# First attention: weighted-value calls placed one at a time behind score and projection calls, with new orders on all four engines

## The chip, the cores and the metric

One core of a Trainium2 chip runs the whole program. The metric is device time in microseconds, the median of several executions.

## What is computed

The reference is a two-layer transformer with modulated layer norms. Only its first attention is touched by the change. It works on 32 samples of 256 tokens by 128 features, with 16 query heads and 8 key heads of 64 features (two query heads share one key head):

```python
h = _layernorm(x) * (1 + ca) + sa
x1 = _rmsnorm(h, norm_w)
q, k, v = heads(x1 @ Wq), heads(x1 @ Wkv[:, :512]), heads(x1 @ Wkv[:, 512:])
q, k = _mh_rmsnorm(q, q_gamma), _mh_rmsnorm(k, k_gamma)     # per head
sim = tanh(q @ k.T / 50) * 50 / sqrt(64)                     # causal mask
out = sum over the two query heads of softmax(sim) @ v       # per key head
x = x + ga * (merge(out) @ Wout)
```

A mixture-of-experts layer, a second attention and a second feed-forward part follow. They are the same before and after the change.

## The kernel before

The function `attention0` (L297) holds the stage. Its unit of work is one **sample** n: two tiles (t = 0, 1) of 128 tokens. Each engine runs a loop over n written out by hand, in which it works on several samples at once: while the scores of sample n are made, the projections of n+2, the transposes of n+1 and the end of n-1 are done. There is no order except the one written in these loops, and each engine executes its own list strictly in that order. Semaphore waits (`wait_ge`) in each helper tie the engines together. The steps of a sample are these:

- **TensorE** (PE). `pe_transpose_x` turns the modulated input, `pe_project_qk` (L432, m = 0 to 5) and `pe_values` (L402) multiply with the weights (float32, 512 columns). `pe_turn_k` (L444) and `pe_turn_q` (L460) turn keys and queries, eight float16 transposes each. `pe_scores` (L476) makes the score products of one of four **groups** g of four query heads in the three-bank PSUM tile `pS`, as eight float16 calls of 512 or 256 columns. `pe_weighted_values` (L491, L492) makes the weighted values of one **pair** p of query heads (two pairs to a group): six float32 calls, whose stationary operand is a 128x128 block of the probabilities `pr` and whose moving operand is `va`, 66 columns wide (64 values and the row sum). A float32 matmul shows in the trace as two records, each with its own weight load. `pe_heads_back` (L513), `pe_out_project` (L529) and `pe_out_back` (L543) end the sample.
- **ScalarE** (ACT). `act_square_qk` (L869) squares a projection, `act_hi` (L879) makes the high float16 half of the normalised keys (u = 0) or queries (u = 1), `act_take_values` (L922), `act_take_k` (L885) and `act_take_heads` (L909) copy from PSUM, `act_tanh` (L897) and `act_exp` (L903) work on one group of scores.
- **VectorE** (DVE). `dve_gain` (L698) applies the gammas, `dve_sums` (L704) and `dve_factors` (L719 to L738) make the inverse norms, `dve_norm` (L745) multiplies them into `qg`, in SBUF, in place. `lower` (L759) makes the low float16 half: of keys on VectorE, of queries on GpSimd, each reading the high half that ScalarE made. `dve_outputs` (L750, L754) divides a pair by its row sums, `dve_take_q` (L767) copies turned queries from PSUM, `dve_normalise` (L680) and `dve_ln` (L638 to L652) prepare later samples, `dve_add` (L128) and `dve_measure` (L136, L140) end an earlier one.
- **GpSimd** (POOL). `gp_mask` (L982) sets the masked probabilities of a group to zero in two instructions, `gp_sum` (L990) adds the two query heads of a pair, `lower` (L759) makes the low half of the queries, and `gp_modulate` (L998, L1000) the modulated input.
- **SyncE** (SP) copies the turned keys into a second tile with the halves exchanged (`k2`, L373 and L374), for which the scores wait.

In the order before, all six calls of a pair stand in one block:

```python
for gg in range(G2):
    hh = p % 2 * G2 + gg
    for t in range(TT):
        out = pO[p % 2][:, (t * G2 + gg) * VW:(t * G2 + gg + 1) * VW]
        pe.matmul(out, w[:, hh * N + t * P:hh * N + (t + 1) * P], v[:, 0, p, :], start=True, stop=t == 0)
    last = pe.matmul(out, w[:, HPG * N + hh * P:HPG * N + (hh + 1) * P], v[:, 1, p, :], start=False, stop=True)
last.then_inc(s_pv, 1)
```

and the scores of a group are followed by both pairs of the same group. On VectorE, the lower half of the keys and the normalising of a later sample come in the order `dve_outputs(n, 1)`, `dve_normalise(n + 3)`, `lower(n + 1, 0, 0)`, `lower(n + 1, 0, 1)`. On ScalarE the high half of the keys comes first and that of the queries after it; on GpSimd `lower(n + 1, 1, 0)` and `lower(n + 1, 1, 1)` have the mask of group 2 between them.

## Time and profile before

| | us |
|---|---|
| median of 3 runs | 2014.13 (2013.62 to 2015.25) |
| profiled execution, first to last instruction | 2010.0 |
| median less that span | 4.1 |
| PE busy in the span | 1952.2 (97%) |
| DVE busy in the span | 1615.3 (80%) |
| ACT busy in the span | 1449.2 (72%) |
| POOL busy in the span | 691.0 (34%) |
| first attention: first and last PE record of L389 and L543 | 18.4 to 955 |

The profiled execution's own time is its span and what lies around it; the trace covers the span alone. Busy time of an engine is the union of its instructions. Consecutive instructions of VectorE and ScalarE overlap in the trace by about 0.08 and 0.12 us, so a queue advances by less than the printed durations. Matmul ends are modelled, and of TensorE it is the start of one record after another that tells how fast it goes. The granted TensorE clock is 1.00 in every stretch from 50 to 900 us.

### The profile page before, as it was taken

The page shows a single profiled execution, that of the slowest core. Times are in us where ns is not written, and L with a number is a line of the kernel's source. Part 1 is how long each engine was busy: PE and PEld are TensorE (multiplying, and loading weights), DVE is VectorE, ACT ScalarE, POOL GpSimd, SP SyncE. Part 2 cuts the span into 40 slices and gives each one's busy share as a digit, 9 for nine tenths or more (in the row PEclk, how much of TensorE's full clock was granted, in tenths as well). Part 3 has the DMA queues.
Part 4 walks back from the last instruction along what each step waited for, and adds up shares of the span by engine and source line. Part 5 has one row for each costly group of instructions (what it writes and reads, how often), then busy time and mean ns, then how long its engine had stood idle before and what let it go on. Part 6 is the DMA issues. An engine that isn't in the chain of part 4 may idle for free. (4 is left out here: it accounts for less than half of the span.)

```text
span 2010.0 us, 39988 instructions
## 1 busy us (share of the span) xinstructions
PE 1952.2 (97%) x14366; PEld 1295.0 (64%) x14366; DVE 1615.3 (80%) x3897; ACT 1449.2 (72%) x2052; POOL 691.0 (34%) x956
## 2 busy tenths in 40 slices
PE   7999999999999999999899999899999997999998
PEld 4777777777777777778444444677777763444443
DVE  6888888888888888874777776688888887888886
ACT  4877888788878887786577777566666664676765
POOL 1545554555555554554000000255555550000000
PEclk8999999999999999999899999999999998999999
DMA  3501110111011100100486655100000000000000
GB/s 98 123 17 27 28 27 14 27 28 27 15 27 27 27 18 24 27 22 12 86 185 128 126 105 110 44 2 2 2 2 2 2 2 1 17 11 16 11 17 16
DMA packets 56995, 75.58 MB, mean 38 GB/s; under 512 B 9456, under 2 KB 34144, under 8 KB 56672
## 3 DMA queue, kind: packets, MB, share of 16 engines
q1 hardware_dynamic: 56800, 73.03, 15.4%
q8 instruction: 116, 1.90, 0.4%
q14 instruction: 79, 0.65, 0.1%
HBM read 51.47 MB, written 4.77 MB: 28 GB/s over the span
## 5 line engine op out<-in xcount | busy, mean ns | idle before, releaser
L982 POOL TENSOR_SCALAR_AFFINE_SELECT pr<-pr 128x512 f32<-128x512 f32 x256 | 202.1, 813 | 315.4 <-ACT pr L903 315.4
L491 PE MATMUL a_pO<-va,pr 128*128 128x66 f32 x2048 | 302.8, 270 | 0.8 <-POOL pr L982 0.4
L491 PEld LDWEIGHTS a_pO<-va,pr 128*128 128x128 f32 x2048 | 271.8, 192 | 17.8 <-issue 15.5
L1871 ACT ACTIVATE c_pr<-c_pS 128x1536 f32<-128x1536 f32 x128 | 185.8, 1451 | 105.6 <-PE c_pS L1669 105.6
L1915 POOL TENSOR_SCALAR_AFFINE_SELECT c_pr<-c_pr 128x512 f32<-128x512 f32 x256 | 175.7, 714 | 129.0 <-DVE c_pr L1759 129.0
L897 ACT ACTIVATE th<-a_pS 128x1536 f32<-128x1536 f32 x128 | 185.9, 1453 | 29.6 <-PE a_pS L476 29.6
L869 ACT ACTIVATE sq<-a_pW 128x512 f32<-128x512 f32 x192 | 114.3, 597 | 128.4 <-PE a_pW L432 123.9
L492 PE MATMUL a_pO<-va,pr 128*128 128x66 f32 x1024 | 198.0, 275 | 0.0
L903 ACT ACTIVATE pr<-th 128x1536 f32<-128x1536 f32 x128 | 190.4, 1488 | 3.1
L476 PE MATMUL a_pS<-qs,k 128*128 128x512 f16 (+1 forms) x1024 | 187.3, 326 | 0.9 <-issue 0.9
L1189 PE MATMUL b_pD<-b_a,b_dn 128*128 128x512 f32 x320 | 164.5, 600 | 3.7 <-DVE b_a L1339 3.2
L1759 DVE TENSOR_SCALAR c_pr<-c_pr 128x1536 f32<-128x1536 f32 x128 | 130.0, 1016 | 43.4 <-ACT c_pr L1871 43.3
L1179 PE MATMUL b_pU<-b_hT,b_un 128*128 128x512 f32 x320 | 163.7, 597 | 0.0
L476 PEld LDWEIGHTS a_pS<-qs,k 128*128 128x128 f16 x1024 | 98.6, 98 | 99.9 <-issue 35.9
L492 PEld LDWEIGHTS a_pO<-va,pr 128*128 128x128 f32 x1024 | 155.5, 192 | 0.0
L698 DVE TENSOR_TENSOR qg<-a_pW,a_gam 128x512 f32<-128x512 f32 x192 | 130.1, 679 | 26.8 <-ACT sq L869 26.8
L990 POOL TENSOR_TENSOR as<-on 128x128 f32<-128x128 f32 x256 | 113.8, 455 | 106.0 <-PE a_pW L513 94.5
L1339 DVE TENSOR_TENSOR b_a<-b_q,b_cwB 128x512 f32<-128x512 f32 x128 | 87.5, 688 | 73.1 <-ACT b_q L1430 57.2
L1417 ACT ACTIVATE b_r<-b_pU 128x512 f32<-128x512 f32 x160 | 95.6, 597 | 67.6 <-PE b_pU L1179 67.6
L759 POOL TENSOR_TENSOR qp<-qg,qp 128x1024 f16<-128x1024 f32 x64 | 137.1, 2142 | 15.0 <-ACT qp L879 15.0
L750 DVE RECIPROCAL rl<-a_pO 128x4 f32<-128x4 f32 x256 | 44.6, 174 | 118.3 <-PE a_pO L492 118.3
L432 PE MATMUL a_pW<-a_wq,hT 128*128 128x512 f32 x256 | 123.6, 605 | 2.0 <-DVE qs L767 1.4
(264 smaller groups left out, 4354.6 us busy)
## 6 DMA issues: line engine op xcount, KB each, us to landing
b_cwB<-b_by_expert SPq DMA_DIRECT2D x64, 512.0 KB, 8.4
k<-k SPq DMA_DIRECT2D x64, 256.0 KB, 3.7
x<-in_L_attn_tokens_dram SPq DMA_DIRECT2D x8, 512.0 KB, 7.0
out_dram<-x SPq DMA_DIRECT2D x16, 256.0 KB, 2.3
mb<-a_by_sample SPq DMA_DIRECT2D x31, 128.0 KB, 3.5
d_h<-in_L_ffn_h_w_dram SPq DMA_DIRECT2D x2, 1024.0 KB, 8.3
c_gb<-c_by_sample SPq DMA_DIRECT2D x1, 2048.0 KB, 7.2
b_by_expert<-b_cwT SPq DMA_DIRECT2D x64, 8.0 KB, 1.4
```

The costliest lines, as they stand in the source:

```text
L476: last = pe.matmul(out, kk[:, h // G2, keys * P:(keys + 1) * P], qs[k][:, h:h + G2, keys * P:N], start=first, stop=not first)
L491: pe.matmul(out, w[:, hh * N + t * P:hh * N + (t + 1) * P], v[:, 0, p, :], start=True, stop=t == 0)
L492: last = pe.matmul(out, w[:, HPG * N + hh * P:HPG * N + (hh + 1) * P], v[:, 1, p, :], start=False, stop=True)
L698: dve.tensor_tensor(qg[n % 2][:, t, cols], pW[BANK_OF[m]][:, :], gam[:, cols], ALU.mult).then_inc(s_qg, 1)
L759: eng.tensor_tensor(to[:, t, :, DH:2 * DH], x.rearrange('p (h d) -> p h d', d=DH), to[:, t, :, 0:DH], ALU.subtract).then_inc(done, 1)
L897: act.activation(th[:, :], pS[:, :], ACT.Tanh, scale=1.0 / SOFTCLAMP).then_inc(s_th, 1)
L903: act.activation(pr[g % 2][:, :], th[:, :], ACT.Exp, scale=SOFTCLAMP * DH ** (-0.5)).then_inc(s_pr, 1)
L982: last = gp.affine_select(out=part, in_=part, compare_op=ALU.is_ge, fill=0.0, base=0, pattern=[[0, HPG], [1, P]], channel_multiplier=-1)
L1179: pe.matmul(pU[(IT * n + u) % 4][:, :], uT[:, t, :], hT[n % 3][:, :], start=True, stop=True).then_inc(s_up, 1)
L1189: pe.matmul(pD[:, :], dT[:, t * D:(t + 1) * D], a[(IT * n + u) % 4][:, :], start=u == 0, stop=u == IT - 1).then_inc(s_dn, 1)
L1871: act.activation(pr[g][:, :, :], pS[:, :, 0:N + P], ACT.Exp, scale=float(1.0 / np.sqrt(np.float32(DQ)))).then_inc(s_ex, 1)
L1915: last = gp.affine_select(out=part, in_=part, compare_op=ALU.is_ge, fill=0.0, base=0, pattern=[[0, HPG], [1, P]], channel_multiplier=-1)
```

## The change

The six calls of a pair become separate calls (`pe_weigh`), as do the score products (`pe_score`), which are now twelve calls of 256 columns to a group in place of four of 512 and four of 256. The transposes and the output projection of the end of a sample are split in the same way. In the new TensorE order most weighted-value calls stand between two score calls, and they belong to the group that was scored two groups earlier. Each PSUM bank of `pW` gets new tenants, with other waits (`pe_turn_k(n, 1)` now waits for `dve_take_q(n, 0)`). The semaphore of the high halves is split into one for keys and one for queries, and the orders of ScalarE, VectorE and GpSimd are written anew; each loop runs one turn longer. In `dve_ln` the steps 2 and 3 exchange their work. Left out below are the old orders (they stand in the listing above), the `if not 0 <= n < B: return` lines and waits of other helpers; indentation is cut by one or two levels.

```diff
-BANK_OF = (0, 1, 2, 1, 0, 2)
-QT_BANK = (1, 0, 0, 2)
+QK_BANK = (1, 2, 0, 0, 1, 2)
+QT_BANK = (2, 1, 2, 2)
+KT_BANK, V_BANK, HB_BANK = (1, 2), (1, 2), (2, 0)
+X_BANK, O_BANK, BACK_BANK = 1, 0, 0
+SCORES, PAIR_CALLS = 12, 6
 SAMPLES_OF_LOAD = B // X_LOADS
...
+s_hi = [sem(x) for x in ('hik', 'hiq')]
...
 def pe_turn_k(pe, n, t):
+    if not 0 <= n < B:
+        return
     pe.wait_ge(s_lo, 2 * n + t + 1)
-    if n >= 2:
-        pe.wait_ge(s_at, 2 * n - 3 + t)
-    elif t:
-        pe.wait_ge(s_va, 2 * n + 2)
+    if t == 0:
+        pe.wait_ge(s_va, 2 * n + 1)
     else:
-        pe.wait_ge(s_qg, 6 * n + 8)
-    out = pW[1 - t][:, :].bitcast(F16)
+        pe.wait_ge(s_qs, 4 * n + 1)
+    out = pW[KT_BANK[t]][:, :].bitcast(F16)
     for p in range(KH):
         last = pe.transpose(out[:, p * P:(p + 1) * P], kp[:, t, p, :], c.id16[:, :])
...
+def pe_score(pe, n, g, m):
+    if not 0 <= n < B:
+        return
     k = n % 2
+    if m == 0:
+        if g == 0:
+            pe.wait_ge(s_qs, 4 * n + 2)
+            pe.wait_ge(s_k2, 32 * (n + 1))
+        elif g == 2:
+            pe.wait_ge(s_qs, 4 * n + 4)
+        if n or g:
+            pe.wait_ge(s_th, 4 * n + g)
+    hh, part = m // 6 * G2, m % 2
+    keys = m % 6 // 4
+    h = g * HPG + hh
+    if keys:
+        out, q = pS[:, HPG * N + hh * P:HPG * N + (hh + G2) * P], qs[k][:, h:h + G2, P:N]
+    else:
+        hh, h = hh + m % 6 // 2, h + m % 6 // 2
+        out, q = pS[:, hh * N:(hh + 1) * N], qs[k][:, h, :]
+    last = pe.matmul(out, (k1, k2)[part][k][:, h // G2, keys * P:(keys + 1) * P], q, start=part == 0, stop=part == 1)
+    if m == SCORES - 1:
+        last.then_inc(s_sc, 1)
+
+def pe_weigh(pe, n, g, call):
+    if not 0 <= n < B:
+        return
+    p, k = 2 * g + call // PAIR_CALLS, call % PAIR_CALLS
+    if k == 0:
+        if p == 0:
+            pe.wait_ge(s_va, 2 * n + 2)
+        pe.wait_ge(s_mk, 4 * n + g + 1)
+        if n or p >= 2:
+            pe.wait_ge(s_on, 8 * n + p - 1)
     w, v = pr[g % 2], va[n % 2]
+    gg, part = k // 3, k % 3
+    t = min(part, 1)
+    hh = p % 2 * G2 + gg
+    out = pO[p % 2][:, (t * G2 + gg) * VW:(t * G2 + gg + 1) * VW]
+    if part < 2:
+        last = pe.matmul(out, w[:, hh * N + t * P:hh * N + (t + 1) * P], v[:, 0, p, :], start=True, stop=t == 0)
+    else:
         last = pe.matmul(out, w[:, HPG * N + hh * P:HPG * N + (hh + 1) * P], v[:, 1, p, :], start=False, stop=True)
+    if k == PAIR_CALLS - 1:
+        last.then_inc(s_pv, 1)
+
...
+    pe.wait_ge(s_as, 8 * n + 2 * j + 2)
...
+    for n in range(-3, B + 2):
+        for m in range(9, 12):
+            pe_score(pe, n, 0, m)
+            pe_weigh(pe, n - 1, 2, m - 2)
+        pe_project_qk(pe, n + 2, 0)
+        pe_weigh(pe, n - 1, 2, 10)
+        pe_project_qk(pe, n + 2, 1)
+        pe_weigh(pe, n - 1, 2, 11)
+        if n == B:
+            for m in range(0, 3):
+                pe_turn_following(pe, m)
+        for m in range(0, 10):
+            pe_score(pe, n, 1, m)
+            pe_weigh(pe, n - 1, 3, m)
+        pe_score(pe, n, 1, 10)
+        pe_score(pe, n, 1, 11)
+        pe_weigh(pe, n - 1, 3, 10)
+        pe_project_qk(pe, n + 2, 2)
+        pe_weigh(pe, n - 1, 3, 11)
+        pe_values(pe, n + 1, 0)
+        if n == B:
+            for m in range(3, 6):
+                pe_turn_following(pe, m)
+        pe_heads_back(pe, n - 1, 0, 0)
+        pe_heads_back(pe, n - 1, 0, 1)
+        pe_score(pe, n, 2, 0)
+        pe_heads_back(pe, n - 1, 0, 2)
+        pe_score(pe, n, 2, 1)
+        pe_weigh(pe, n, 0, 0)
+        pe_score(pe, n, 2, 2)
+        pe_weigh(pe, n, 0, 1)
+        pe_score(pe, n, 2, 3)
+        pe_heads_back(pe, n - 1, 0, 3)
+        pe_score(pe, n, 2, 4)
+        pe_weigh(pe, n, 0, 2)
+        pe_score(pe, n, 2, 5)
+        pe_heads_back(pe, n - 1, 1, 0)
+        pe_score(pe, n, 2, 6)
+        pe_weigh(pe, n, 0, 3)
+        pe_score(pe, n, 2, 7)
+        pe_heads_back(pe, n - 1, 1, 1)
+        pe_score(pe, n, 2, 8)
+        pe_heads_back(pe, n - 1, 1, 2)
+        pe_score(pe, n, 2, 9)
+        pe_heads_back(pe, n - 1, 1, 3)
+        pe_score(pe, n, 2, 10)
+        pe_weigh(pe, n, 0, 4)
+        pe_values(pe, n + 1, 1)
+        pe_weigh(pe, n, 0, 5)
+        if n == B:
+            pe_turn_following(pe, 6)
+            keep_busy(pe, c, pO[0], 6)
+        pe_out_project(pe, n - 1, 0)
+        pe_weigh(pe, n, 0, 6)
+        pe_out_project(pe, n - 1, 1)
+        pe_weigh(pe, n, 0, 7)
+        pe_score(pe, n, 2, 11)
+        pe_weigh(pe, n, 0, 8)
+        pe_out_project(pe, n - 1, 2)
+        pe_weigh(pe, n, 0, 9)
+        pe_out_project(pe, n - 1, 3)
+        pe_weigh(pe, n, 0, 10)
         if n == -1:
             keep_busy(pe, c, pS, 14)
+        pe_turn_k(pe, n + 1, 0)
+        pe_weigh(pe, n, 0, 11)
+        if n == -1:
+            keep_busy(pe, c, pS, 8)
+        pe_turn_q(pe, n + 1, 0)
+        pe_weigh(pe, n, 1, 0)
+        for m in range(0, 5):
+            pe_score(pe, n, 3, m)
+            pe_weigh(pe, n, 1, m + 1)
         if n == -1:
             keep_busy(pe, c, pS, 10)
+        pe_turn_k(pe, n + 1, 1)
+        pe_score(pe, n, 3, 5)
+        pe_weigh(pe, n, 1, 6)
+        pe_score(pe, n, 3, 6)
+        pe_project_qk(pe, n + 2, 3)
+        pe_weigh(pe, n, 1, 7)
+        pe_score(pe, n, 3, 7)
         if n == -1:
             keep_busy(pe, c, pS, 8)
+        pe_turn_q(pe, n + 1, 1)
+        pe_score(pe, n, 3, 8)
+        pe_weigh(pe, n, 1, 8)
+        pe_score(pe, n, 3, 9)
+        pe_weigh(pe, n, 1, 9)
+        pe_turn_q(pe, n + 1, 2)
+        pe_score(pe, n, 3, 10)
+        pe_weigh(pe, n, 1, 10)
+        pe_score(pe, n, 3, 11)
+        pe_weigh(pe, n, 1, 11)
+        pe_project_qk(pe, n + 2, 4)
+        pe_weigh(pe, n, 2, 0)
+        pe_project_qk(pe, n + 2, 5)
         if n < -1:
             keep_busy(pe, c, pS, (5, 2)[n + 3])
+        pe_out_back(pe, n - 1, 0)
+        pe_score(pe, n + 1, 0, 0)
+        pe_out_back(pe, n - 1, 1)
+        for m in range(1, 4):
+            pe_score(pe, n + 1, 0, m)
+            pe_weigh(pe, n, 2, m)
+        pe_score(pe, n + 1, 0, 4)
+        pe_transpose_x(pe, n + 3, 0)
+        pe_score(pe, n + 1, 0, 5)
+        pe_weigh(pe, n, 2, 4)
+        pe_score(pe, n + 1, 0, 6)
+        pe_transpose_x(pe, n + 3, 1)
         if n < -1:
             keep_busy(pe, c, pS, (4, 7)[n + 3])
+        pe_score(pe, n + 1, 0, 7)
+        pe_weigh(pe, n, 2, 5)
+        pe_score(pe, n + 1, 0, 8)
+        pe_weigh(pe, n, 2, 6)
+        pe_turn_q(pe, n + 1, 3)
...
-    elif step == 2:
+    elif step == 3:
...
 def lower(eng, n, u, t, done):
-    eng.wait_ge(s_hi, 4 * n + 2 * u + t + 1)
+    if not 0 <= n < B:
+        return
+    eng.wait_ge(s_hi[u], 2 * n + t + 1)
...
+    for n in range(-3, B + 2):
+        dve_take_q(dve, n, 1)
+        dve_take_q(dve, n, 2)
+        dve_ln(dve, n + 2, 0)
+        dve_gain(dve, n + 1, 3)
+        dve_ln(dve, n + 2, 1)
+        dve_outputs(dve, n - 1, 3)
+        dve_gain(dve, n + 1, 4)
+        dve_gain(dve, n + 1, 5)
+        dve_sums(dve, n + 1, 1)
+        dve_mean_square(dve, n + 1)
+        dve_take_q(dve, n, 3)
+        dve_outputs(dve, n - 1, 4)
+        dve_add(dve, n - 2)
+        dve_factors(dve, n + 1, 0)
+        dve_outputs(dve, n - 1, 5)
+        dve_gain(dve, n + 2, 0)
+        dve_gain(dve, n + 2, 1)
+        dve_ln(dve, n + 2, 2)
+        dve_outputs(dve, n - 1, 6)
+        dve_factors(dve, n + 1, 1)
+        dve_outputs(dve, n - 1, 7)
+        dve_gain(dve, n + 2, 2)
+        dve_norm(dve, n + 1, 0)
+        dve_norm(dve, n + 1, 1)
+        dve_outputs(dve, n, 0)
+        lower(dve, n + 1, 0, 0, s_lo)
+        dve_normalise(dve, n + 3)
+        dve_measure(dve, n - 2, 1)
+        lower(dve, n + 1, 0, 1, s_lo)
+        dve_outputs(dve, n, 1)
+        dve_measure(dve, n - 2, 2)
         if n == B:
             dve.wait_ge(s_st, ADD_STEPS * (B - 1))
             ln_scales(dve, c, s_ls, 0, slice(0, TILES - TT))
+        dve_take_q(dve, n + 1, 0)
+        dve_sums(dve, n + 2, 0)
+        dve_outputs(dve, n, 2)
+        dve_ln(dve, n + 2, 3)
     dve.wait_ge(s_st, ADD_STEPS * B)
...
+    for n in range(-3, B + 2):
+        act_square_qk(act, n + 2, 0)
+        act_square_h(act, n + 2, 0)
+        act_square_qk(act, n + 2, 1)
+        act_exp(act, n, 0)
+        act_square_h(act, n + 2, 1)
+        act_tanh(act, n, 1)
+        act_square_qk(act, n + 2, 2)
+        act_exp(act, n, 1)
         if n == B:
+            for m in range(0, 6):
                 act_take_following(act, m)
+        act_take_heads(act, n - 1, 0)
+        act_take_values(act, n + 1, 0)
+        act_take_heads(act, n - 1, 1)
+        act_hi(act, n + 1, 1, 0)
+        act_hi(act, n + 1, 0, 0)
+        act_hi(act, n + 1, 0, 1)
+        act_take_values(act, n + 1, 1)
+        act_tanh(act, n, 2)
+        act_hi(act, n + 1, 1, 1)
         if n == B:
             act_take_following(act, 6)
+        act_gate(act, n - 1)
+        act_take_k(act, n + 1, 0)
+        act_take_k(act, n + 1, 1)
+        act_exp(act, n, 2)
+        act_square_qk(act, n + 2, 3)
+        act_tanh(act, n, 3)
+        act_square_qk(act, n + 2, 4)
+        act_square_qk(act, n + 2, 5)
+        act_exp(act, n, 3)
+        act_turned(act, n + 3)
+        act_tanh(act, n + 1, 0)
...
+    for n in range(-3, B + 2):
+        gp_sum(gp, n - 2, 6)
+        gp_sum(gp, n - 2, 7)
+        gp_mask(gp, n - 1, 1)
+        lower(gp, n, 1, 0, s_ql)
+        gp_sum(gp, n - 1, 0)
+        lower(gp, n, 1, 1, s_ql)
+        gp_sum(gp, n - 1, 1)
+        gp_mask(gp, n - 1, 2)
+        gp_modulate(gp, n + 2)
+        gp_sum(gp, n - 1, 2)
+        gp_mask(gp, n - 1, 3)
+        gp_sum(gp, n - 1, 3)
+        gp_sum(gp, n - 1, 4)
+        gp_mask(gp, n, 0)
+        gp_sum(gp, n - 1, 5)
 MOE_LOADS = 6
```

## Rows read from the trace of the kernel before

**Rows 1.** The page: span, TensorE, and one DMA (KB each, us to landing).

```profile
span 2010.0 us, 39988 instructions
...
PE 1952.2 (97%) x14366; PEld 1295.0 (64%) x14366; DVE 1615.3 (80%) x3897; ACT 1449.2 (72%) x2052; POOL 691.0 (34%) x956
...
k<-k SPq DMA_DIRECT2D x64, 256.0 KB, 3.7
```

**Rows 2.** Windows, first and last of six (PE, PEld, DVE, ACT, POOL busy, PEclk).

```profile
200.00:300.00 100.00, 100.00 (x759) 77.97 (x759) 83.11 (x191) 83.40 (x107) 57.21 (x73) 1.00 0.11 27
...
700.00:800.00 100.00, 100.00 (x735) 76.22 (x734) 85.76 (x195) 80.98 (x108) 50.57 (x68) 1.00 0.09 21
```

**Rows 3.** Timeline of PE, one sample: start us, length us, line, operation, count.

```profile
388.11 0.38 PE L389 MATMUL a_pW<-id,hm 128*128 128x128 f32 x2
...
401.92 1.46 PE L476 MATMUL a_pS<-qs,k 128*128 128x512 f16 x8
403.22 0.56 PE L491 MATMUL a_pO<-va,pr 128*128 128x66 f32 x4
...
403.84 0.61 PE L491 MATMUL a_pO<-va,pr 128*128 128x66 f32 x4
...
406.24 0.61 PE L444 MATMUL a_pW<-id,kp 128*128 128x128 f16 x8
406.69 1.95 PE L529 MATMUL a_pW<-at,a_wo 128*128 128x256 f32 x8
408.47 0.61 PE L444 MATMUL a_pW<-id,kp 128*128 128x128 f16 x8
...
416.58 0.38 PE L389 MATMUL a_pW<-id,hm 128*128 128x128 f32 x2
```

**Rows 4.** Timeline of DVE and POOL near the stage start, where they meet.

```profile
60.94 1.12 DVE L680 TENSOR_SCALAR a_xn<-x,mv,rr 128x128 f32<-128x128 f32 x2
...
64.01 1.69 DVE L759 TENSOR_TENSOR kp<-qg,kp 128x512 f16<-128x512 f32 x1
...
58.94 2.62 POOL L982 TENSOR_SCALAR_AFFINE_SELECT pr<-pr 128x512 f32<-128x512 f32 x2 [4.34 <-ACT pr L903]
61.53 0.86 POOL L990 TENSOR_TENSOR as<-on 128x128 f32<-128x128 f32 x2
63.02 2.14 POOL L759 TENSOR_TENSOR qp<-qg,qp 128x1024 f16<-128x1024 f32 x1 [0.62 <-ACT qp L879]
```

**Rows 5.** Timeline of DVE, the same sample as rows 3.

```profile
396.92 1.75 DVE L745 TENSOR_TENSOR qg<-qg,rr 128x1536 f32<-128x1536 f32 x1
398.58 0.68 DVE L698 TENSOR_TENSOR qg<-a_pW,a_gam 128x512 f32<-128x512 f32 x1
...
402.18 0.59 DVE L680 TENSOR_SCALAR a_xn<-x,mv,rr 128x128 f32<-128x128 f32 x2
402.69 0.68 DVE L759 TENSOR_TENSOR kp<-qg,kp 128x512 f16<-128x512 f32 x1
...
407.21 1.05 DVE L649 TENSOR_SCALAR ss<-ag 128x2 f32<-128x2 f32 x1
...
412.26 1.28 DVE L767 COPY qs<-a_pW 128x1024 f16<-128x1024 f16 x2
```

**Rows 6.** Timeline of POOL, the same sample.

```profile
399.46 2.74 POOL L982 TENSOR_SCALAR_AFFINE_SELECT pr<-pr 128x512 f32<-128x512 f32 x2 [4.23 <-ACT pr L903]
...
406.10 2.14 POOL L759 TENSOR_TENSOR qp<-qg,qp 128x1024 f16<-128x1024 f32 x1
408.18 1.23 POOL L982 TENSOR_SCALAR_AFFINE_SELECT pr<-pr 128x512 f32<-128x512 f32 x2
```

**Rows 7.** Timeline of ACT, the same sample.

```profile
402.88 1.06 ACT L879 ACTIVATE qp<-qg 128x1024 f16<-128x1024 f32 x1
403.83 1.46 ACT L897 ACTIVATE th<-a_pS 128x1536 f32<-128x1536 f32 x1
...
405.64 1.50 ACT L903 ACTIVATE pr<-th 128x1536 f32<-128x1536 f32 x1
```

More of the change, by code:

```diff
@@ new lines, in pe_heads_back @@
+        def pe_heads_back(pe, n, t, j):
+            if not 0 <= n < B:
+                return
+            pe.wait_ge(s_as, 8 * n + 2 * j + 2)
+            if j == 0:
+                if t == 0:
+                    if n + 3 < B:
+                        pe.wait_ge(s_qg, 6 * n + 20)
+                    elif n + 1 < B:
+                        pe.wait_ge(s_qs, 4 * n + 8)
+                    else:
+                        pe.wait_ge(s_at, 2 * n - 1)
+                else:
+                    if n + 3 < B:
+                        pe.wait_ge(s_qg, 6 * n + 21)
+                    else:
+                        pe.wait_ge(s_st, 3 * n - 2)
+            last = pe.transpose(pW[HB_BANK[t]][:, j * P:(j + 1) * P], as_[:, t, j * P:(j + 1) * P], c.id32[:, :])
+            if j == KW // P - 1:
+                last.then_inc(s_aT, 1)
@@ L532, in pe_turn_following, with pe_out_project @@
+        def pe_out_project(pe, n, j):
+            if not 0 <= n < B:
+                return
+            if j == 0:
+                pe.wait_ge(s_at, 2 * n + 2)
+                if n == 0:
+                    pe.wait_ge(weights.s_loaded, 16 * ATTENTION0_LOADS)
+                pe.wait_ge(s_at, 2 * n + 2)
+            last = pe.matmul(pW[O_BANK][:, 0:N], wo[:, j, :], at[:, j, :], start=j == 0, stop=j == KW // P - 1)
+            if j == KW // P - 1:
+                last.then_inc(s_o, 1)
         def pe_turn_following(pe, m):
@@ L538, in pe_turn_following, with pe_out_back @@
             moe_turn(pe, c, following, m, pS[:, m % 3 * BANK:(m % 3 + 1) * BANK]).then_inc(s_turned, 1)
-        def pe_out_back(pe, n):
-            pe.wait_ge(s_og, n + 1)
-            for t in range(TT):
-                last = pe.transpose(pW[2][:, t * P:(t + 1) * P], og[:, t * P:(t + 1) * P], c.id32[:, :])
-            last.then_inc(s_oT, 1)
+        def pe_out_back(pe, n, t):
+            if not 0 <= n < B:
+                return
+            if t == 0:
+                pe.wait_ge(s_og, n + 1)
+                if n + 3 < B:
+                    pe.wait_ge(s_qg, 6 * n + 22)
+                else:
+                    pe.wait_ge(s_og, n + 1)
+            last = pe.transpose(pW[BACK_BANK][:, t * P:(t + 1) * P], og[:, t * P:(t + 1) * P], c.id32[:, :])
+            if t == TT - 1:
+                last.then_inc(s_oT, 1)
         @block.tensor
@@ L671, in dve_normalise @@
         def dve_normalise(dve, n):
+            if not 1 <= n < B:
+                return
             if n >= 2:
@@ L689, in dve_gain @@
         def dve_gain(dve, n, m):
+            if not 0 <= n < B:
+                return
             t, b = m // 3, OF_BLOCK[m]
@@ L706, in dve_factors @@
         def dve_factors(dve, n, part):
+            if not 0 <= n < B:
+                return
             base = 9 * n
@@ L740, in dve_norm @@
         def dve_norm(dve, n, t):
+            if not 0 <= n < B:
+                return
             dve.wait_ge(s_f, 9 * n + 9)
@@ L761, in dve_take_q @@
         def dve_take_q(dve, n, i):
+            if not 0 <= n < B:
+                return
             j, t = i // 2, i % 2
@@ L899, in act_exp @@
         def act_exp(act, n, g):
+            if not 0 <= n < B:
+                return
             act.wait_ge(s_th, 4 * n + g + 1)
@@ L905, in act_take_heads @@
         def act_take_heads(act, n, t):
+            if not 0 <= n < B:
+                return
             if t == 0 and n >= 1:
@@ L916, in act_take_values @@
         def act_take_values(act, n, t):
+            if not 0 <= n < B:
+                return
             if t == 0:
@@ L985, in gp_sum @@
         def gp_sum(gp, n, p):
+            if not 0 <= n < B:
+                return
             gp.wait_ge(s_on, 8 * n + p + 1)
@@ L992, in gp_modulate @@
         def gp_modulate(gp, n):
+            if not 1 <= n < B:
+                return
             gp.wait_ge(s_xn, n)
```

427 lines of the change are left out of this document (101 added, 326 removed).

## The prediction

> **What bounds the kernel now.** The page gives a span of 2010.0 us and TensorE busy for 97% of it [rows 1]. I read the windows next: in six stretches of 100 us from 200 to 800 TensorE is busy all the time at clock 1.00, VectorE 83 to 86%, ScalarE 80 to 83%, GpSimd 51 to 57% [rows 2]. So the order of before never makes TensorE wait in the steady state. The timeline then gives the length of a sample: L389 comes 28.47 us after itself, 388.11 to 416.58 [rows 3]. 28 samples have that length; what TensorE needs for one sample is what counts.
>
> Where TensorE's time goes is read from starts, not durations [rows 3]. Eight score calls, four of 512 and four of 256 columns, take 403.22 - 401.92 = 1.30 us, so 0.216 and 0.109 us each. Eight float16 transposes of 128 columns take 0.45 us, 0.056 each. Eight float32 records of 256 columns take 408.47 - 406.69 = 1.78 us: 8 x 0.216 and 0.05 once. A weighted-value record has only 66 columns, yet six of them take 403.84 - 403.22 = 0.62 us: five of 0.112, and one, the first behind the scores, of 0.06. (The first four last 0.56 us, the next four 0.61.) I read this so: a float32 weight load takes 0.112 us and can hide behind the call ahead of it. Behind another 66-column record, whose own pass takes 0.058, 0.054 us stick out. Ahead of the L529 block the same 0.05 sticks out behind a 0.056 us transpose. The load of a float16 call is short enough for 0.056.
>
> **The change on TensorE.** A weighted-value call is two records. Alone it costs 2 x 0.112 = 0.224; with a float16 call behind it the last record costs 0.058, together 0.170. I counted the records of a turn of the loop by what follows. Before, 90 of the 96 weighted-value records stand ahead of a float32 load that sticks out, after 59: 31 x 0.054 = 1.67 us gained. Float16 transposes with such a load behind them go from 4 to 2: 0.11 gained. Score columns are the same (12 x 256 against 4 x 512 + 4 x 256); 33 more changes from scores to a load of 0.112 behind 0.109 cost 0.09. Net 1.69: TensorE could do a sample in 28.47 - 1.69 = **26.78 us**. The sum of all records at these prices gives 28.45 for the order of before, 0.02 off. The clock stays at 1.00 as long as TensorE is this busy; no row shows it lower at 97%.
>
> The bounds of this term are zero (if a float16 load sticks out too) and 2 x 33 x 0.054 = 3.5 us (if both loads hid); I take 1.69, since both prices are in [rows 3]. [...]
>
> **What has to keep up.** VectorE's queue, 0.84 x 28.47 = 24.0 us, and ScalarE's, 23.3, fit into 26.78. I laid the new orders beside TensorE's, with time 0 at the first score call of a turn n: 0.11 for a score, 0.17 or 0.22 for a weighted-value call, 0.86 for a projection. Group 1's last score starts at 5.90, heads-back (1,3) at 10.71, `turn_k(n+1, 0)` at 15.08, `turn_q(n+1, 0)` at 15.75, `turn_k(n+1, 1)` at 17.82. The waits on tanh have 0.6 to 0.9 us to spare. The key copy DMA has none: 3.7 us from issue to landing [rows 1], with two issues ahead about 4.35 us after `take_k`, where 4.4 are left; I price it at zero, up to 0.2.
>
> **The term that decides** is a lock between VectorE and GpSimd. In [rows 4] the two L680 take 1.12 us where they take 0.59 elsewhere [rows 5]: the first ends 0.08 after the mask (61.56), the second 0.08 after L990's first instruction. L759 on VectorE takes 1.69 instead of 0.68 and ends 0.55 after GpSimd's L759 (65.16). In the steady state L649, two elements wide, takes 1.05 until GpSimd's L759 ends (408.24), and a mask takes 2.74 instead of 1.23 behind an L745 [rows 5, 6]. At each end the one that waits gets in first, so they alternate. Instructions that read PSUM (L750, L754, L767) run beside GpSimd. Before, `normalise` and the key `lower` at 402.69 fall where GpSimd is idle, behind the mask that ends at 402.20 [rows 5, 6]. The Trainium skill, "SBUF — State Buffer", section "Who interferes with whom", says that VectorE with two SBUF inputs, or in a two-port mode such as `tensor_scalar` can enter, shares a port pair with GpSimd and the second to issue blocks fully. The trace agrees.
>
> The new order sets these instructions against each other. The steps:
> - 6.21 tanh of group 1 starts (0.31 after its score). Square of projection 2 from 7.55 (0.60 us), gain 8.19 (0.68 [rows 5]), `norm(.,0)` 8.79 to 10.54 (1.75 us).
> - Exp (1.50 [rows 7]) ends 9.52 and the mask of group 1 asks at 9.59. It alternates with the norms: part one ends 11.03, `norm(.,1)` 12.64, part two 13.13, where 10.8 would stand without the lock.
> - ScalarE: heads 11.03, query half 11.5, key halves 12.45 and 12.97, values 13.5, tanh of group 2 at 14.06, second query half 15.39 to 16.46 (an instruction's length less 0.12 of overlap, as 402.88 + 1.06 stands to 403.83 [rows 7]).
> - GpSimd's query `lower` starts at 13.1 and ends 15.22 (2.14). VectorE's key `lower` asks at 13.13, ends 15.77: `turn_k(.,0)`, due 15.08, waits **0.74**.
> - GpSimd's sum ends 16.08, `normalise` 16.16 and 16.42, `measure` runs to 16.8, the second key `lower` asks at **16.73**. GpSimd's second query `lower` is ready at **16.53** and has nothing ahead of it. It takes the lock to 18.66; the key `lower` ends 19.2.
> - Queued behind it: `outputs(n,1)` to 19.8, `measure`, `take_q(.,0)` to 20.5. `turn_k(.,1)` waits for both of them and starts at 20.57, not 17.82: **2.75 us** in all, the 0.74 in it. Behind it wait the rest of the scores, which wait for nothing later.
>
> 26.78 + 2.75 = **29.5 us** a sample, 1.05 more than 28.47. Over 28 samples 29.4. Lead-in and drain: the last sample's score groups need tanh between them, and twelve score calls with twelve weighted-value calls take 3.4 us where a block took 1.3, so up to 4 x 2.1; some 16 calls of those turns gain. I price both ends together at +2 (0 to 6). 29.4 + 2 = 31 on the profiled execution's 2010.0, 2041; the median stands 4.1 above that span: **2045 us**.
>
> **Rivals.** *The key half gets in first* (0.25). The two requests are 0.20 us apart at the end of a chain of some fifteen steps; this is the point that decides. If the key `lower` asks first, it ends at 17.4 or earlier, `take_q` at 18.5 to 18.7, and 0.7 to 0.9 us remain as a stall: 27.6 us a sample, 28 x 0.87 = 24 less, plus 2: **1992**. For it: the lead is small, and one request more or less at 13.1 removes it. Against: the key `lower` is two `normalise`, two `measure` and a wait behind, every turn alike.
> *The plan holds* (0.18). The lock costs less than read (say because the norms or the query half fall elsewhere) and 26.8 to 26.9 hold: 28 x 1.63 = 46 less, plus 2: **1970**. For it: all the rest of the timetable fits closely. Against: [rows 4].
> *Some turns go one way, some the other* (0.06): between 2000 and 2030. *More waits than seen*, as the key copy or group 2's mask (0.03): 2060 to 2075.
> The change does what it says in each of them; that the calls are not covered at all is excluded by [rows 3].
>
> **How the numbers follow.** Forecast 0.48. 0.2% is 4 us, about what a measurement of this kernel can tell. Faster 0.25 + 0.18 + 0.03 = 0.46, slower 0.48 + 0.03 = 0.51, same 0.03. The forecast's own range is 2030 to 2056 (a stall of 2.3 to 3.1 us a sample and the ends). Both signs hold much of the chance, and leaving out the plan's case would leave out more than 2 in 10, so the whole range is 1966 to 2056.
>
> **What the profile after would show.** Right: TensorE idle once a sample, ahead of L444's second block, ended by VectorE's L767 of `take_q` or its L759; GpSimd's L759 and VectorE's L759 overlapping, the latter 2 us and more long; a sample of 29.5 us; weighted-value records 0.06 and 0.112 apart in turn behind scores. Wrong: TensorE again 100% in 200 to 800 (the plan), or VectorE's second L759 at 0.68 us (the first rival). A sample other than 26.78 plus TensorE's idle time would say that the cover was mispriced.

## The result, and the profile after

The changed kernel takes **2080.99 us** (median of 4 runs, 2079.70 to 2082.19), the kernel before 2013.88 us on the same chip (4 runs, 2011.86 to 2015.25). The ratio is 1.0335, with a 95% interval of 1.0322 to 1.0348: 3.3% slower. The forecast was slower by 31 us; it is 67 us.

The page of the changed kernel, the lines that answer to [rows 1]:

```profile
span 2078.8 us, 41395 instructions
...
PE 1942.7 (93%) x14878; PEld 1337.0 (64%) x14878; DVE 1730.8 (83%) x3897; ACT 1435.2 (69%) x2052; POOL 738.6 (36%) x956
...
k<-k SPq DMA_DIRECT2D x64, 256.0 KB, 3.7
```

TensorE has 512 more records and is busy for 10 us less in a span that is 69 us longer. The windows, answering to [rows 2] (length, then PE, PEld, DVE, ACT and POOL busy, and PEclk):

```profile
200.00:300.00 100.00, 92.57 (x750) 76.33 (x750) 90.94 (x188) 74.12 (x100) 54.22 (x68) 0.97 0.08 21
700.00:800.00 100.00, 92.00 (x741) 76.14 (x740) 91.38 (x173) 76.04 (x101) 57.16 (x65) 0.97 0.08 21
```

Two things are new in these rows: TensorE stands for 7 to 8% of the time where it never stood, and its granted clock is 0.97 where it was 1.00. Which wait it is, the waits view of the stretch from 200 to 800 tells (who waited <- who released it: us in total, times, longest us):

```profile
DVE qs L863 <- PE a_pW L481: 36.0, 41, 2.2
PE a_pW L460 <- DVE qs L863: 36.0, 19, 1.9
...
PE a_pW L460 <- DVE kp L853: 11.7, 20, 0.6
```

L460 is the turned keys' transpose (L444 before), L853 the low halves (`lower`, L759 before), L863 `take_q` (L767). Each turn TensorE stands twice: 0.6 us ahead of block 0, put down to the key `lower`, and 1.9 us ahead of block 1, put down to `take_q`. (The first line is VectorE standing ahead of later `take_q`s, whose transposes come late behind TensorE's own stand.) The timeline of one sample shows what is behind it (start us, length us, engine, line, operation, count, and in brackets the idle time before). First TensorE, a sample that begins at 505.85 (L395, `transpose_x`, answers to L389 of [rows 3]):

```profile
505.85 0.27 PE L395 MATMUL a_pW<-id,hm 128*128 128x128 f32 x1
...
522.41 0.33 PE L524 MATMUL a_pO<-va,pr 128*128 128x66 f32 x2
523.33 0.62 PE L460 MATMUL a_pW<-id,kp 128*128 128x128 f16 x8 [0.58 <-DVE kp L853]
...
525.91 0.34 PE L526 MATMUL a_pO<-va,pr 128*128 128x66 f32 x2
528.15 0.61 PE L460 MATMUL a_pW<-id,kp 128*128 128x128 f16 x8 [1.90 <-DVE qs L863]
...
535.42 0.27 PE L395 MATMUL a_pW<-id,hm 128*128 128x128 f32 x1
```

Then VectorE and GpSimd in the same turn, answering to [rows 5, 6] and to the meeting in [rows 4]:

```profile
516.28 3.85 DVE L835 TENSOR_TENSOR qg<-qg,rr 128x1536 f32<-128x1536 f32 x2
...
520.61 2.66 DVE L853 TENSOR_TENSOR kp<-qg,kp 128x512 f16<-128x512 f32 x1
523.20 0.73 DVE L760 TENSOR_SCALAR a_xn<-x,mv,rr 128x128 f32<-128x128 f32 x2
...
524.25 2.47 DVE L853 TENSOR_TENSOR kp<-qg,kp 128x512 f16<-128x512 f32 x1
526.64 0.17 DVE L842 RECIPROCAL rl<-a_pO 128x4 f32<-128x4 f32 x1
...
527.34 0.66 DVE L863 COPY qs<-a_pW 128x1024 f16<-128x1024 f16 x1
```

```profile
517.08 3.54 POOL L1058 TENSOR_SCALAR_AFFINE_SELECT pr<-pr 128x512 f32<-128x512 f32 x2 [0.95 <-ACT pr L990]
520.60 2.12 POOL L853 TENSOR_TENSOR qp<-qg,qp 128x1024 f16<-128x1024 f32 x1
522.69 0.90 POOL L1068 TENSOR_TENSOR as<-on 128x128 f32<-128x128 f32 x1
524.04 2.13 POOL L853 TENSOR_TENSOR qp<-qg,qp 128x1024 f16<-128x1024 f32 x1 [0.45 <-ACT qp L958]
```

GpSimd's first query `lower` starts at 520.60, VectorE's key `lower` 0.01 us behind it; the key half takes 2.66 us and ends 0.55 us after GpSimd's. The second time GpSimd starts at 524.04 and VectorE asks at 524.25, and again the key half takes 2.47 us where 0.68 was the length alone [rows 5]. On VectorE `outputs` and `take_q` queue behind it; `take_q` ends at 528.00, and block 1 of the keys starts at 528.15.

**Where the 69 us went.** From L395 to L395 this sample is 29.57 us. But only some of the turns are that long: of the 28 in the stage 17 last 31.1 to 31.2 us, and the other eleven 27.5 to 30.4. The stretch behind the stand of a longer one, in the windows view:

```profile
579.00:589.20 10.20, 7.72 (x69) 6.78 (x68) 10.13 (x15) 6.84 (x10) 7.96 (x6) 1.00 0.00 0
589.20:592.60 3.40, 3.40 (x17) 2.31 (x15) 1.84 (x4) 2.73 (x3) 0.33 (x1) 0.50 0.20 45
592.60:602.00 9.40, 9.40 (x83) 7.63 (x82) 8.22 (x19) 6.12 (x8) 4.83 (x9) 1.00 0.23 57
```

and TensorE in it:

```profile
588.94 0.83 PE L460 MATMUL a_pW<-id,kp 128*128 128x128 f16 x8 [1.90 <-DVE qs L863]
...
590.31 1.92 PE L448 MATMUL a_pW<-a_wq,hT 128*128 128x512 f32 x2
```

where the sample shown above has, at the same place of the turn,

```profile
528.98 1.02 PE L448 MATMUL a_pW<-a_wq,hT 128*128 128x512 f32 x2
```

After the stand of 1.90 us the granted clock is 0.50 for 3.4 us, the lower of TensorE's two levels (1.2 GHz), and the two records of a projection take 1.92 us where they take 1.02 at full clock. The fall begins 22.0 to 23.0 us into the turn in all 17 of them, near the end of the second stand or just behind it; it costs 31.22 - 29.57 = 1.65 us. (The Trainium skill, "TensorE: Matmul & The Clock Gate", section "Terms", sets the penalty at the throttled time times the share of pulses left out, an estimate of 3.4 x 0.5 = 1.7 us here; the trace agrees.) In the kernel before the clock was 1.00 through all of these turns. So the difference of the spans, 2078.8 - 2010.0 = 68.8, divides into:
- the 28 turns, 855.95 us against 796.98: 59.0. Of it 17 x 1.65 = 28.1 is the clock, and 30.9 (1.10 a turn) the stands less what the cover gives back.
- the lead-in: the first L395 of these turns starts at 79.38 us instead of 75.03, 4.3.
- from the last L395 to the end: 1143.5 us instead of 1138.0, 5.5. Of it 4.7 lie in the rest of the first attention (88.0 us instead of 83.3 to the last record of L580, L543 before) and 0.8 behind it.

### The profile page after: what moved, and what is told of

Same layout as the page of the kernel before. It is cut to its first block and busy times, and to the rows that moved or that the text cites. A ratio compares the mean times of both kernels' runs of the same rounds, so it can differ in the third digit from the quotient of the medians.

```text
span 2078.8 us, 41395 instructions
## 1 busy us (share of the span) xinstructions
PE 1942.7 (93%) x14878; PEld 1337.0 (64%) x14878; DVE 1730.8 (83%) x3897; ACT 1435.2 (69%) x2052; POOL 738.6 (36%) x956
## 5 line engine op out<-in xcount | busy, mean ns | idle before, releaser
L504 PE MATMUL a_pS<-qs,k 128*128 128x256 f16 x1536 | 400.2, 277 | 8.5 <-issue 4.3
L524 PEld LDWEIGHTS a_pO<-va,pr 128*128 128x128 f32 x2048 | 329.2, 195 | 62.2 <-issue 48.7
L1058 POOL TENSOR_SCALAR_AFFINE_SELECT pr<-pr 128x512 f32<-128x512 f32 x256 | 227.5, 912 | 327.6 <-ACT pr L990 327.6
L524 PE MATMUL a_pO<-va,pr 128*128 128x66 f32 x2048 | 339.0, 254 | 1.3 <-POOL pr L1058 1.3
L504 PEld LDWEIGHTS a_pS<-qs,k 128*128 128x128 f16 x1536 | 206.9, 136 | 22.6 <-issue 20.1
L526 PEld LDWEIGHTS a_pO<-va,pr 128*128 128x128 f32 x1024 | 162.0, 191 | 43.3 <-issue 42.5
L526 PE MATMUL a_pO<-va,pr 128*128 128x66 f32 x1024 | 173.9, 251 | 0.0
L1068 POOL TENSOR_TENSOR as<-on 128x128 f32<-128x128 f32 x256 | 130.0, 513 | 101.6 <-DVE on L846 101.6
L448 PE MATMUL a_pW<-a_wq,hT 128*128 128x512 f32 x256 | 152.0, 681 | 2.3 <-DVE qg L782 1.5
L853 DVE TENSOR_TENSOR kp<-qg,kp 128x512 f16<-128x512 f32 x64 | 152.7, 2386 | 0.1
L853 POOL TENSOR_TENSOR qp<-qg,qp 128x1024 f16<-128x1024 f32 x64 | 138.1, 2158 | 26.5 <-ACT qp L958 26.4
L966 ACT ACTIVATE k<-a_pW 128x1024 f16<-128x1024 f16 x64 | 65.9, 1030 | 111.0 <-PE a_pW L460 111.0
L863 DVE COPY qs<-a_pW 128x1024 f16<-128x1024 f16 x128 | 87.1, 681 | 64.2 <-PE a_pW L481 64.2
```

Of the source, the lines that this page charges most:

```text
L504: last = pe.matmul(out, (k1, k2)[part][k][:, h // G2, keys * P:(keys + 1) * P], q, start=part == 0, stop=part == 1)
L524: last = pe.matmul(out, w[:, hh * N + t * P:hh * N + (t + 1) * P], v[:, 0, p, :], start=True, stop=t == 0)
L853: eng.tensor_tensor(to[:, t, :, DH:2 * DH], x.rearrange('p (h d) -> p h d', d=DH), to[:, t, :, 0:DH], ALU.subtract).then_inc(done, 1)
L1058: last = gp.affine_select(out=part, in_=part, compare_op=ALU.is_ge, fill=0.0, base=0, pattern=[[0, HPG], [1, P]], channel_multiplier=-1)
```

## The experiments

The theory after the result has three parts. (1) TensorE's own work is about 26.78 us a sample, because a weighted value's load hides behind a wide call. (2) It stands 2.81 us because VectorE's key `lower` lies in turn behind GpSimd's query `lower`. (3) The stand lets the clock fall in most turns, about 28 us in all. The rivals are that the calls cost more than 26.78 us and the stand less, that the stand comes from the order of VectorE alone with no part of GpSimd's, and that the clock's fall is only beside the matter. f1_fill, f2_dve, f3_both and f4_half ran on one chip together, beside a before of 2012.83 us (7 runs, 2012.08 to 2014.05); f5_blocks, f6_later and f7_fill9 on another chip, beside a before of 2012.63 us (7 runs, 2010.59 to 2017.09).

**1. The stand filled with work (f1_fill).** 18 transposes that nobody reads, ahead of block 1:

```diff
+                if 0 <= n + 1 < B:
+                    keep_busy(pe, c, pS[:, 2 * N:3 * N], 18)
                 pe_turn_k(pe, n + 1, 1)
```

> Theory (lock, then clock): the wait of 2.06 us ahead of turn_k(n+1, 1) is set by the two lower halves on VectorE and GpSimd, and the idle TensorE of that wait makes the granted clock fall to 0.5 for 3.4 us in about 17 samples, 1.65 us each. 18 filler transposes (0.109 us each, 1.96 us) in the place of the wait leave the wait's end where it is and keep TensorE busy: every sample 29.57 us, clock 1.00 from 200 to 800 us, about 28 us less than the changed kernel: 2053 us. Rival (the samples of 31.2 us are more waits on VectorE and GpSimd, and the clock follows): the samples stay at 30.6 on average, 2078 to 2084 us.

Measured: 2065.98 us (2064.29 to 2067.69), ratio 1.0264 (1.0249 to 1.0280). Twenty of the 28 turns last 29.56 to 29.62 us, and the clock stays at 1.00 in the whole stage. The windows:

```profile
200.00:300.00 100.00, 98.23 (x832) 82.32 (x831) 93.98 (x192) 77.24 (x104) 54.89 (x70) 1.00 0.09 21
```

It follows that the long turns of the change are the clock's doing: work that nobody needs, put into the stand, makes the kernel 15 us faster. The expectation, 2053 us, was missed by 13. Of these 3.5 are a lead-in of 82.89 us instead of 79.38 (the transposes also run in turns that have no stand yet), 2.1 the first turn of the stage, which has no stand in the change (29.56 us instead of 27.50), and 2.2 lie behind the stage. Most of the rest are six turns of 30.3 to 30.7 us, in which the key copy lands late (below), where the change has three. What holds the turn at 29.57 is not touched.

**2. Half of the transposes (f7_fill9).** As f1_fill, with 9:

> The kernel of the change with 9 transposes without use ahead of the second block of turned keys, half of the 18 of f1_fill: they take about 1.1 of the 2.06 us that TensorE stands there, and the other 0.95 us stays idle. The sample's own length should not move (29.57 us without a fall of the clock). Theory A (falls come from the long stand, and a shorter one keeps the clock): granted clock 1.00 in nearly all of the stage, about 2066 us as f1_fill. Theory B (any stand of about 1 us on top of the 0.75 us in front of block 0 lets it fall as often): falls of 3.4 us in half of the samples or more, 2078 to 2083 us. In between, some samples fall and the time lies in proportion to their number, 1.65 us for each.

Measured: 2062.79 us (2059.30 to 2065.68), ratio 1.0248 (1.0232 to 1.0265). TensorE still stands ahead of block 1, half as long, and in no turn of the stage does the clock fall:

```profile
516.84 1.15 PE L119 MATMUL a_pS<-id 128*128 128x128 f32 x9
518.90 0.61 PE L460 MATMUL a_pW<-id,kp 128*128 128x128 f16 x8 [0.91 <-DVE qs L865]
```

This is theory A of the expectation: with a stand of 0.9 us behind one of 0.6 us the clock fell in none of 28 turns, with one of 1.9 us behind one of 0.6 us it fell in 17 of 28. The spans differ by 2078.8 - 2057.5 = 21.3 us: 28 from the clock, of which this version gives back 3.8 in the 28 turns (five last 30.2 to 30.4 us, with a late key copy), 2.5 after the stage and 0.5 ahead of it.

**3. VectorE's order alone (f2_dve).** Both key halves one behind the other, ahead of the measures and `outputs(n, 1)`; `normalise` later:

```diff
                 lower(dve, n + 1, 0, 0, s_lo)
-                dve_normalise(dve, n + 3)
-                dve_measure(dve, n - 2, 1)
                 lower(dve, n + 1, 0, 1, s_lo)
+                dve_measure(dve, n - 2, 1)
                 dve_outputs(dve, n, 1)
                 dve_measure(dve, n - 2, 2)
...
                 dve_sums(dve, n + 2, 0)
+                dve_normalise(dve, n + 3)
                 dve_outputs(dve, n, 2)
```

> VectorE's order alone: the second key lower right behind the first, normalise(n+3) behind the sums. Theory (lock, and who asks first): the second key lower gets the lock before GpSimd's second query lower and ends near 16.6 us of the turn instead of 19.2; turn_k(n+1, 1) waits no more, turn_k(n+1, 0) still 0.75 us: 27.5 to 27.7 us a sample, clock 1.00, 1996 to 2006 us. Rival (VectorE, busy for 90% of the time, is simply too full for this order): still 29 us or more a sample, above 2040 us.

Measured: 1998.97 us (1997.37 to 1999.54), ratio 0.9932 (0.9916 to 0.9949), turns of 27.51 us, clock 1.00. The kernel is now 0.7% faster than before, by the order of a few items on VectorE. The second key half has asked before GpSimd's second query half does:

```profile
535.86 3.53 DVE L853 TENSOR_TENSOR kp<-qg,kp 128x512 f16<-128x512 f32 x2
```

```profile
535.84 2.13 POOL L853 TENSOR_TENSOR qp<-qg,qp 128x1024 f16<-128x1024 f32 x1
539.28 2.13 POOL L853 TENSOR_TENSOR qp<-qg,qp 128x1024 f16<-128x1024 f32 x1 [0.45 <-ACT qp L958]
```

Both key halves take 3.53 us together, one of 2.66 that meets GpSimd and one of 0.94 that doesn't, and the second is over when GpSimd's second starts. The wait ahead of block 1 is gone; that ahead of block 0 is as it was:

```profile
538.58 0.62 PE L460 MATMUL a_pW<-id,kp 128*128 128x128 f16 x8 [0.59 <-DVE kp L853]
```

26.78 + 0.75 = 27.53, and 27.51 was measured. This is what the prediction's first rival describes, made on purpose: the key half gets in first. The Trainium skill, "SBUF — State Buffer", section "Who interferes with whom", puts it as "Issue order, not op shape, decides who blocks", and the runs agree.

**4. The first stand too (f3_both).** In addition the first key half stands ahead of `outputs(n, 0)`, and ScalarE makes the high half of the keys before that of the queries, so that VectorE asks first there as well:

```diff
                 dve_norm(dve, n + 1, 1)
-                dve_outputs(dve, n, 0)
                 lower(dve, n + 1, 0, 0, s_lo)
+                dve_outputs(dve, n, 0)
                 lower(dve, n + 1, 0, 1, s_lo)
...
-                act_hi(act, n + 1, 1, 0)
                 act_hi(act, n + 1, 0, 0)
+                act_hi(act, n + 1, 1, 0)
                 act_hi(act, n + 1, 0, 1)
```

> As the run before, and ScalarE makes the high half of keys 0 ahead of that of queries 0, VectorE's first key lower stands ahead of outputs(n, 0). Theory: both key halves get the lock ahead of GpSimd's query halves, no wait is left at turn_k; a sample takes what TensorE needs, 26.8 us (26.7 to 27.0), VectorE's L853 stays under 1.3 us, 1972 to 1984 us. Rival (the cover of the weight loads is worth less than 1.69 us a sample): TensorE is busy all the time and a sample takes 27.5 us or more, above 1995 us.

Measured: **1979.41 us** (1976.07 to 1980.67), ratio 0.9832 (0.9817 to 0.9846), turns of 26.94 us. TensorE has no stand left:

```profile
200.00:300.00 100.00, 99.87 (x860) 83.29 (x859) 95.14 (x211) 83.56 (x111) 62.75 (x77) 1.00 0.11 28
```

The two engines still meet, but now in this order:

```profile
522.25 1.11 DVE L853 TENSOR_TENSOR kp<-qg,kp 128x512 f16<-128x512 f32 x1
522.86 2.50 POOL L853 TENSOR_TENSOR qp<-qg,qp 128x1024 f16<-128x1024 f32 x1
523.84 2.07 DVE L853 TENSOR_TENSOR kp<-qg,kp 128x512 f16<-128x512 f32 x1
```

The first key half goes ahead, GpSimd's query half takes 2.50 us instead of 2.13, and the second key half, asking at 523.84, gets in when GpSimd ends (525.36) and takes 2.07. Here the expectation missed: both key halves were to be ahead of GpSimd and under 1.3 us each, and only the first is. It costs little, since TensorE waits for it no longer than 0.2 us. It is the change as it could have been: 1.7% faster than the kernel before, with TensorE's new order untouched.

**5. Less work on GpSimd (f4_half).** The kernel of the change in all its orders, GpSimd's query `lower` over half of the heads. It leaves out the low halves of heads 8 to 15, which a `memset` ahead of the loop (not shown) sets to zero; `...` stands for the operands:

```diff
-            eng.tensor_tensor(to[:, t, :, DH:2 * DH], ..., to[:, t, :, 0:DH], ALU.subtract).then_inc(done, 1)
+            hs = slice(0, KH)
+            eng.tensor_tensor(to[:, t, hs, DH:2 * DH], ...[:, hs, :], to[:, t, hs, 0:DH], ALU.subtract).then_inc(done, 1)
```

> The changed kernel with GpSimd's query lower cut to 8 of the 16 heads (the low halves of heads 8 to 15 are left at zero), nothing else moved. Theory (lock): GpSimd's L853-like instruction takes 1.1 instead of 2.1 us, so VectorE's first key lower ends near 14.8 of the turn and the second asks near 15.7, before GpSimd's second is ready at 16.5: both waits ahead of turn_k vanish, 26.8 to 27.1 us a sample, 1974 to 1986 us. Rival (the waits come from VectorE's own queue or from PSUM banks): 29.5 to 31 us a sample as in the changed kernel, since VectorE's work is the same.

Measured: 1975.04 us in a single run, turns of **26.78 us**. VectorE's queue is the one of the change, item by item; only GpSimd's instruction is shorter:

```profile
520.78 1.15 POOL L854 TENSOR_TENSOR qp<-qg,qp 128x512 f16<-128x512 f32 x1
520.80 1.69 DVE L854 TENSOR_TENSOR kp<-qg,kp 128x512 f16<-128x512 f32 x1
...
523.46 0.67 DVE L854 TENSOR_TENSOR kp<-qg,kp 128x512 f16<-128x512 f32 x1
524.22 1.16 POOL L854 TENSOR_TENSOR qp<-qg,qp 128x512 f16<-128x512 f32 x1 [1.43 <-ACT qp L959]
```

The first key half still waits out GpSimd's (1.69 us, over 0.56 after it), the second meets nothing and takes 0.67 us. With 1 us less of GpSimd's work in front of each key half, both stands are gone but for 0.04 us. That rules out that VectorE's order is too long by itself. It also measures TensorE's own term, 26.74 us and the 0.04, within a few hundredths of the forecast.

**6. The cover taken away (f5_blocks).** The kernel of f3_both, with the four loops that alternate scores and weighted values pulled apart (one of them shown):

```diff
                 for m in range(0, 10):
                     pe_score(pe, n, 1, m)
+                for m in range(0, 10):
                     pe_weigh(pe, n - 1, 3, m)
```

> The kernel of f3_both with the order of TensorE changed in its four loops that alternate a score product and a weighted value: each loop now gives all its scores first and then all its weighted values, (9,12), (0,10), (0,5) and (1,4). Nothing else moves, every call and transfer is the same. Theory (a weighted value behind a wide call costs 0.054 us less than one behind another weighted value, because its first load lies beside the call): 2 + 9 + 4 + 2 = 17 covers are lost, 17 x 0.054 = 0.92 us a sample, so 27.8 to 27.9 us a sample against the 26.94 of f3_both and about 2005 us in all. Rival (the gain of the new order lies elsewhere, for instance in when the groups come due, and the covers are worth nothing or half): 26.9 to 27.4 us a sample, 1979 to 1992 us. A second rival (the blocks also put calls in front of their inputs): over 28 us a sample with a wait in front of a score or a weighted value that f3_both does not have.

Measured: 1999.75 us (1998.78 to 2000.22), ratio 0.9937 (0.9920 to 0.9953), turns of 27.62 us. The longest loop in it:

```profile
524.99 1.26 PE L504 MATMUL a_pS<-qs,k 128*128 128x256 f16 x10
526.09 0.56 PE L524 MATMUL a_pO<-va,pr 128*128 128x66 f32 x4
526.48 0.39 PE L526 MATMUL a_pO<-va,pr 128*128 128x66 f32 x2
...
528.27 0.38 PE L504 MATMUL a_pS<-qs,k 128*128 128x256 f16 x2
```

Ten scores start 0.110 us apart (1.10 us), and the 20 records of the ten weighted-value calls behind them take 528.27 - 526.09 = 2.18 us: the first 0.06 and each of the others 0.112, so 0.109 on average. Where they alternate, as in f3_both,

```profile
507.37 0.27 PE L504 MATMUL a_pS<-qs,k 128*128 128x256 f16 x1
...
507.48 0.34 PE L526 MATMUL a_pO<-va,pr 128*128 128x66 f32 x2
...
507.65 0.27 PE L504 MATMUL a_pS<-qs,k 128*128 128x256 f16 x1
```

a pair takes 0.17 us, 0.086 a record. The cover is real, but the expectation was 0.24 us a turn too high. It set 0.92 on top of 26.94; but TensorE, slower now, no longer waits ahead of block 1, where f3_both waits 0.20 us and f4_half 0.04 (below), so the base is 26.74. 27.62 - 26.74 = 0.88 for 17 lost covers is 0.052 each, against 0.054 forecast. The short records, 0.06 us to the next start, are 46 of 96 in a turn of f3_both and 29 here: 17 fewer.

**7. One weighted value later (f6_later).** In f3_both the waits view puts 5.3 us down to GpSimd's mask, ahead of the first weighted value of group 2:

```diff
                 pe_project_qk(pe, n + 2, 4)
-                pe_weigh(pe, n, 2, 0)
                 pe_project_qk(pe, n + 2, 5)
                 if n < -1:
                     keep_busy(pe, c, pS, (5, 2)[n + 3])
+                pe_weigh(pe, n, 2, 0)
```

> The kernel of f3_both with one call of TensorE moved: the first weighted value of group 2 stands behind projection 5 in place of between projections 4 and 5. In f3_both it waits 0.2 us in every sample for GpSimd's mask of that group (5.3 us in 22 waits of the stretch from 200 to 800). Theory (that wait is the main part of what keeps the sample at 26.94 where TensorE's own work is 26.78): 26.78 us a sample, about 5 us less in all, 1974 us. Rival (it is the late landing of the key copy and the wait for the score bank that keep it): 26.9 us and 1978 to 1980 us, the wait on the mask gone all the same.

Measured: 1981.48 us (1980.21 to 1983.51), ratio 0.9846 (0.9831 to 0.9861), turns of 26.94 us as in f3_both. A miss, and one of reading. (The rival has the turn right, 26.9 us, but not the cause, as the rows below show.) The two lines of f3_both,

```profile
PEld a_pO L524 <- issue: 26.8, 112, 0.2
...
PEld a_pO L524 <- POOL pr L1058: 5.3, 22, 0.2
```

become one:

```profile
PEld a_pO L524 <- issue: 31.6, 132, 0.2
```

The 0.24 us ahead of that load is what every load behind a projection record has; the mask had come at about the same time and lent it its name. What does keep f3_both at 26.94 is block 1 of the keys:

```profile
527.35 0.34 PE L526 MATMUL a_pO<-va,pr 128*128 128x66 f32 x2
527.72 0.61 PE L460 MATMUL a_pW<-id,kp 128*128 128x128 f16 x8
```

Its first record starts 0.31 us after the last weighted value (whose second record starts at 527.41). In f4_half it is 0.15 us, in f5_blocks 0.11. That is the difference of 0.16. In the timeline it goes back to the second key half of 2.07 us above, behind which `take_q` ends at 527.57; in f4_half that half takes 0.67 us.

## Why the prediction was right and wrong, step by step

**Right: the sign, the mechanism and its length.** The cover on TensorE: forecast 26.78 us a sample, measured 26.78 in f4_half (that it agrees to the hundredth is luck, see below). The lock: the two requests were forecast 0.20 us apart with GpSimd first (16.53 and 16.73), they are 0.21 apart (524.04 and 524.25). The stands were forecast as 0.74 and 2.01 us; the starts show 523.33 - 522.47 - 0.11 = 0.75 and 528.15 - 525.98 - 0.11 = 2.06 (the second record of a pair starts 0.06 to 0.07 after the first). 26.78 + 2.81 = 29.59, a turn without a fall of the clock has 29.57, and the forecast was 29.53. For 28 turns the forecast was 29.4 us and it is 30.9. The first rival had its turn right too: f2_dve gives 27.51 us where it said 27.6, and 1999 us in all where it said 1992, because both ends are longer (below). The bound at which the term is zero (a float16 load sticks out too) is not borne out either: 26.78 us a turn were reached.

**Right by luck: the two decimals of 26.78.** The prediction has the last record of a weighted-value call short when a float16 call stands behind it, and counts 59 records of 0.112 us. The trace has it the other way round: in f3_both the two records of a call start at 507.48 and 507.54 and the next score at 507.65, so the first is short, 0.06 us, behind a wide call, and the last takes 0.112 although a float16 call follows. By that 50 of the 96 records cost 0.112 in the new order (90 before, as counted), and the weighted values of a turn go from 10.41 to 8.36 us (f4_half): 2.05 gained, not 1.67. Against it stand 0.21 for the projections (5.21 to 5.42 us) and 0.16 for the output projection (1.78 to 1.94), whose second record now sticks out behind a weighted-value call: 0.483 us instead of 0.429, and 0.270 instead of 0.216. The prediction prices neither, and has 0.02 of gain left from two small terms. Two errors of nearly the same size cancel. (Its upper bound, 2 x 33 x 0.054, is 3.6, not 3.5.)

**Wrong: the clock.** "The clock stays at 1.00 as long as TensorE is this busy; no row shows it lower at 97%." This was said of the kernel before, and then used for a forecast in which TensorE stands 2.8 us of every 29.5. The sentence has a condition, and the forecast itself broke it. The clock falls to 0.50 in 17 of 28 turns, 28 us, nearly as much as the stall. It is most of the 36 us by which 2045 was short: 28.1 here, 7.8 from the ends (below), 1.5 from the stands, and -1.9 because the median stands 2.2 above the profiled span (2080.99 and 2078.8) where 4.1 were added. So the step that failed is this term, which the sum has at nothing; the runs show 28 us in its place. It should have stood there with bounds: from zero to a fall in every turn, 28 x 1.65 = 46 us.

**Wrong in size: the two ends.** Forecast +2 (0 to 6), measured 4.3 + 5.5 = 9.8 us. In the lead-in (20 to 50 us) the clock is 0.84 where it was 0.97 before, and TensorE waits 4.7 us at once for the key `lower`. Behind the stage, 1142.6 to 1146.1 us are measured in all versions with the new order of TensorE, stalled or not, against 1138.0: this part goes with the order itself. The weighted values come two groups behind the scores, and the last sample has none to put between. Which of its waits makes how much of it was not tried.

**The key copy** was priced at zero, up to 0.2. In most turns that holds. But every turn that is 0.5 to 1.1 us longer than its neighbours without a fall of the clock has a late landing: three in the change, five in f7_fill9, six in f1_fill, four in f3_both (a fifth, 0.4 us longer, has its issue 0.4 us later). In f3_both, the turn of 27.76 us from 318.59 (the two transfers' time from issue to landing; what TensorE waits for):

```profile
DMA to landing us min/median/max: 4.0/4.3/4.6
```

```profile
PE a_pS L504 <- issue: 0.7, 1, 0.7
```

and a turn of 26.94 us, from 373.29, in which TensorE waits for no score call:

```profile
DMA to landing us min/median/max: 3.2/3.5/3.8
```

The second transfer lands 0.8 us later, and the score call that reads it starts that much later. In the kernel before transfers of 4.6 us occur too, and no turn shows it: there was room. The price was right for the usual landing and too low for one turn in five to nine, about 3 us in all in the change and in f3_both.

The traces also show what comes together with a late landing. In all nine, 41 of the 252 turns of the stage have a landing of 4.1 us or more, and in 35 of these one packet of 16 KB, on a queue of the kind "instruction", starts 0.9 to 2.0 us after the first of the two issues. Of the other 211 turns one has such a packet there, and its landing takes 4.0 us. No run moved or removed those packets, and the six late landings without one stay unexplained.

**The range** reached to 2056 because a stall of at most 3.1 us a turn was taken as the worst. It counted how long TensorE stands, and not what standing does to the work after it.
